# A graph layer with a mixture of experts on one core: three sweeps over the experts with carried places, and results weighed by ScalarE

## What is computed

```python
def layer(x, src, dst, edge_weight, ...):        # x: 3125 x 256, float32; 53125 edges, sorted by dst
    support = layernorm(x) @ weight               # 256 x 256
    msgs = support[src] * edge_weight[:, None]
    x = x + segment_sum(msgs, dst) + bias
    y = layernorm(x)
    top_w, top_i = top_k(y @ Wg + bg, 2)          # 8 experts, each row goes to two
    top_w = softmax(top_w)
    for e in range(8):                            # W1: 256 x 1024, W2: 1024 x 256
        h = gelu(y @ W1[e] + b1[e])
        x = x + w_dense[:, e:e+1] * (h @ W2[e] + b2[e])
    return x
```

## Time and profile before

| | us |
|---|---|
| median of 3 runs | 967.78 |
| lowest, highest | 967.74, 975.76 |
| the profiled execution, time | 968.8 |
| the profiled execution, span from first to last instruction | 967.0 |

### The profile page before, as it was taken

One profiled execution on the slowest core, in us unless ns is written; L12 is line 12 of the kernel. 1 busy time (PEld: TensorE's weight loads), 2 busy tenths in 40 slices (PEclk: granted clock), 3 DMA queues, 4 the chain that ended last, 5 costly groups with the idle time before them and its releaser, 6 DMA issues.

```text
span 967.0 us, 16433 instructions
## 1 busy us (share of the span) xinstructions
PE 783.5 (81%) x5365; PEld 764.0 (79%) x5365; DVE 424.2 (44%) x1229; ACT 307.8 (32%) x594; POOL 585.8 (61%) x570
## 2 busy tenths in 40 slices
PE   1076769966975865399999999999996999999994
PEld 0075768866875764399999999899985999999994
DVE  6422223321331336033655376254634466566653
ACT  5200100200100000124433425344732466666652
POOL 4477777777777777777777777704005255555422
PEclk9999999999999999999999899899988999999998
DMA  8888789753465494436465564714213465666632
GB/s 210 249 291 291 254 270 296 208 158 106 140 175 154 116 267 129 119 116 223 118 222 162 187 189 149 243 42 132 76 55 104 115 164 130 157 173 174 168 56 39
DMA packets 104892, 160.22 MB, mean 166 GB/s; under 512 B 18146, under 2 KB 82131, under 8 KB 104680
## 3 DMA queue, kind: packets, MB, share of 16 engines
q0 software_dynamic: 34688, 69.13, 26.4%
q1 hardware_dynamic: 53988, 64.24, 22.4%
q10 hardware_dynamic: 16132, 25.81, 8.3%
HBM read 107.42 MB, written 51.61 MB: 164 GB/s over the span
## 4 chain that ended last, share of the span: by engine, by line
PE 63%; POOL 11%; DMA 10%; DVE 7%; issue 6%; ACT 1%; DVEq 0%; ACTq 0%; POOLq 0%; SPq 0%
PE ps_agg L786 20%; PE ps_o L948 19%; PE ps_h L931 17%; POOL G L578 7%; DMA G<-xn_d,src_t 7%; POOL y_d L591 3%; PE ps_m L843 2%; DVE w_lo L1143 2%; PE ps_o L852 2%; PE ps_y L904 1%; PE ps_y L843 1%; DMA xe_int<-in_src 1%; DMA y_d<-yr,pos_i 1%; DVE G L1413 1%; DVE ost L1342 1%
## 5 line engine op out<-in xcount | busy, mean ns | idle before, releaser
L578 POOL DMA_INDIRECT G<-xn_d,src_t x416 | 417.2, 1003 | 147.0 <-issue 116.2
L786 PEld LDWEIGHTS ps_agg<-S,G 128*128 128x128 f32 x1664 | 295.1, 275 | 93.0 <-issue 85.2
L786 PE MATMUL ps_agg<-S,G 128*128 128x48 f32 x1664 | 297.8, 354 | 86.1 <-DMA G<-xn_d,src_t 84.3
L728 ACT ACTIVATE hf<-ps_h,b_t 128x256 f32<-128x256 f32 x272 | 113.4, 468 | 231.3 <-PE ps_h L931 206.1
L931 PE MATMUL ps_h<-y_hi,w_hi 128*128 128x256 f32 x544 | 161.5, 297 | 3.3 <-DVE y_lo L1324 3.3
L1330 DVE TENSOR_TENSOR h_lo<-hf,h_hi 128x512 fp32r<-128x512 f32 x136 | 93.3, 692 | 157.4 <-ACT h_hi L731 156.0
L931 PE MATMUL ps_h<-y_hi,w_lo 128*128 128x256 f32 x544 | 157.6, 290 | 0.0
L931 PE MATMUL ps_h<-y_lo,w_hi 128*128 128x256 f32 x544 | 156.8, 288 | 0.0
L1111 DVE TENSOR_TENSOR S<-iota_w,rel_t 128x192 f32<-128x192 f32 x104 | 36.9, 361 | 209.7 <-PE ps_agg L786 202.2
L622 POOL DMA_INDIRECT result<-ost,add_i x34 | 57.7, 1698 | 111.1 <-DVE ost L1347 103.9
L948 PE MATMUL ps_o<-w_hi,h_hi 128*128 128x256 f32 x544 | 114.1, 291 | 9.2 <-DVE h_lo L1330 9.1
(11 more groups left out here) (163 smaller groups left out, 630.6 us busy)
## 6 DMA issues: line engine op xcount, KB each, us to landing
w_raw<-in_L_ffn_W ACTq DMA_DIRECT2D x24, 1024.0 KB, 7.7
y_d<-fill SPq DMA_DIRECT2D x14, 896.0 KB
y_d<-fill SPq DMA_DIRECT2D x14, 777.0 KB
G<-xn_d,src_t POOLq DMA_INDIRECT x416, 3.7
yg<-y_d SPq DMA_DIRECT2D x19, 259.0 KB, 3.6
yg<-y_d SPq DMA_DIRECT2D x19, 256.0 KB, 2.8
y_d<-ost SPq DMA_DIRECT2D x17, 256.0 KB
w_raw<-in_L_ffn_W SPq DMA_DIRECT2D x4, 1024.0 KB, 15.1
```

The lines of the kernel that those rows point to most:

```text
L578: pool.indirect_dma_start(G[:, k, :], None, xn_d, bass.IndirectOffsetOnAxis(src_t[:, n, c:c + 1], 0)).then_inc(main.gathered[n % NR], 16)
L728: nc.scalar.activation(hf[:, j % 2, m, :], ps_h[:, j % 2, m * T:(m + 1) * T], ACT.Gelu, bias=b1_t[:, e * KH + c:e * KH + c + 1]).then_inc( ...
L786: return nc.tensor.matmul(ps_agg[:, k // GT % 2, m * WIN:(m + 1) * WIN], G[:, k, m * 128:(m + 1) * 128], S[:, k, :], start=start, stop=stop)
```

## The change

The nodes are in three sets, `((4, 3, 2), (4, 4), (4, 2, 2))`. The first two sweeps do exactly one tile per expert (16 visits): what an expert has over 256 rows stays in the table and is taken up by the next sweep (`run` is carried over, and only raised where an expert has less than its tile). The third sweep does all the rest, at least one tile an expert. All 16 visits are written out and need no numbers from the chip; `sweep_tables` runs once, for the third sweep.

Every tile now carries node and gate weight (`tile_marks` for all). The results of the visits 0 to 14 are multiplied with the gate weight by ACT in the first quarter of the next tile (`weigh`), and stored by SP to a table `r_d`. SP loads them later into the ring G, free by then, and POOL adds them to the output: visits 0 to 4 (`OLD[0]`) between the send of the last chunk but one and the last, visits 5 to 14 in the third sweep, one or two per expert (`OLD_AT`). The combining of set 0 (L610 to L617, L1406 to L1415) is gone. In the third sweep a tile's results are treated after the first step of the next tile, and an expert's weights are split after its predecessor's last tile.

```diff
-CHUNK_BLOCKS = ((4, 4, 3, 2), (4, 4, 4))
+CHUNK_BLOCKS = ((4, 3, 2), (4, 4), (4, 2, 2))
...
+    STILL = len(SETS) - 1
+    NV = STILL * X
+    AHEAD = NV - 1
...
-    PAIRS_AT = (4, 4, 4, 4, 4, 3, 0, 0)
+    PAIRS_AT = (3, 3, 3, 3, 3, 2, 2, 2, 2, 3, 2, 2, 1, 0, 0, 0)
+    LINEAR_AT = {v: CHUNKS[L0 + n] for n, v in enumerate((3, 5, 9, 11, 13))}
+    TURN_AT = {v + 1: c for v, c in LINEAR_AT.items()}
-    SEND_AT = [COMPLETE[c.index] + pairs_beside(c) + 2 for c in CHUNKS[:L0 - 2]] + [U0, U0 + 2]
-    SEND_AT += [min(HEAD_U[e + 1] + 3, NP) for e in TURN_AT]
+    SEND_AT = [COMPLETE[c.index] + pairs_beside(c) + 2 for c in CHUNKS[:L0 - 1]] + [U0 + 1]
+    SEND_AT += [min(HEAD_U[v + 1] + 1, NP) for v in TURN_AT]
+    OLD = (range(0, 5), range(5, AHEAD))
+    OLD_AT = [[v for v in OLD[1] if (v - OLD[1][0]) * X // len(OLD[1]) == i] for i in range(X)]
...
@@ SP @@
+            for v in range(NV):
...
+                if v < X:
+                    fill_rows(sp, SETS[2], v)
+                new_sweep = (v + 2) % X == 0
+                if not new_sweep and v < AHEAD:
+                    place_free(v + 1)
+                    load_tile(first_rows(v + 2))
+                if v < AHEAD:
+                    store_result(v)
+                if HEAD_U[v] == NP and HEAD_U[v - 1] < NP:
+                    sp.wait_ge(main.used, RING + NG * GT)
+                    sp.wait_ge(q.stored, (v + 1) * 16)
+                    load_old(0)
+                if new_sweep:
+                    rows_sent(SETS[(v + 2) // X])
+                    place_free(v + 1)
+                    load_tile(first_rows(v + 2))
...
@@ POOL @@
+            def add_old(n, v):
+                pool.wait_ge(s_old[n], 16 * len(OLD[n]))
+                pool.wait_ge(s_old_i[n], 1)
+                pool.wait_ge(s_old_added, 16 * TH * v)
+                for h in range(TH):
+                    pool.indirect_dma_start(out, bass.IndirectOffsetOnAxis(old_i[:, v, h:h + 1], 0),
+                                            G[:, v * TH + h, :], None, compute_op=ALU.add).then_inc(s_old_added, 16)
...
             for c, a, z in zip(CHUNKS, [0] + SEND_AT, SEND_AT):
                 gather_pairs(a, z)
+                if c is CHUNKS[-1]:
...
+                    for v in OLD[0]:
+                        add_old(0, v)
                 send(c)
...
+            for i, e in enumerate(SWEEP[STILL]):
+                first, end = bounds(pool, e)
+                for h in range(TH):
+                    pool.wait_ge(q.added[h], first * 16)
+                pool.sem_inc(s_go, 1)
+                for v in OLD_AT[i]:
+                    add_old(1, v)
+                pool.wait_ge(s_old_added, 16 * TH * (OLD_AT[i][-1] + 1))
+                with pool.Fori(first, end) as r:
+                    add_tile(r - 1)
+            add_tile(end - 1)
...
@@ ACT @@
+            def weigh(v):
+                act.wait_ge(q.biased, v + 2)
+                act.wait_ge(q.meta, v * 4 + 4)
+                for h in range(TH):
+                    nc.scalar.activation(ost[:, h, :], ost[:, h, :], ACT.Identity,
+                                         scale=w_tab[:, v, h:h + 1]).then_inc(q.weighed, 1)
...
@@ DVE, place_rows @@
+                for s in SETS[:STILL]:
+                    if c is s.last:
+                        own(V.scalar_tensor_tensor(out=run[:, :], in0=room_row[:, :], scalar=float((s.index + 1) * T),
+                                                   in1=run[:, :], op0=ALU.add, op1=ALU.max))
...
@@ DVE, third sweep @@
+                with dve.Fori(first, end) as r:
+                    g = r + AHEAD
+                    hidden_low(g, 0)
+                    results_to_add(r - 1)
+                    for j in range(1, NQ):
+                        hidden_low(g, j)
+                    tile_low(g + 1)
```

More of the change, by code:

```diff
@@ L48, with __init__ @@
 class NodeSet:
-    def __init__(self, index, chunks, tile, experts):
+    def __init__(self, index, chunks, nodes_up_to, tile):
         self.index, self.chunks = index, chunks
[L53 to L56, removed]
+        self.last = chunks[-1]
+        self.room = index + -(-nodes_up_to // tile)
 class ChunkSems:
@@ new lines, in rows_sent, with first_rows, place_free, store_result @@
+            def rows_sent(s):
+                for c in s.chunks:
+                    sp.wait_ge(ch.sent[c.index], 32 * c.blocks)
+            def first_rows(v):
+                row = (VISITS[v] * ROOM + v // X) * T
+                return slice(row, row + T)
+            def place_free(n):
+                sp.wait_ge(q.tile_t, n + 1)
+                sp.wait_ge(q.meta, n * 4 + 3)
+            def store_result(v):
+                sp.wait_ge(q.weighed, (v + 1) * TH)
+                sp.dma_start(r_d[v * T:(v + 1) * T, :].rearrange("(h p) d -> p h d", p=128),
+                             ost[:, :, :]).then_inc(q.stored, 16)
@@ new lines, in _ @@
+            sp.wait_ge(q.route, 1)
+            row = tile_row(2)
+            place_free(NV)
+            load_tile(bass.ds(row, T))
+            sp.wait_ge(q.stored, NV * 16)
+            load_old(1)
+            for e in SWEEP[STILL]:
+                first, end = bounds(sp, e)
+                with sp.Fori(first, end) as r:
+                    row = tile_row(r + 2)
+                    place_free(r + AHEAD + 1)
+                    load_tile(bass.ds(row, T))
+            sp.wait_ge(q.tile_in, (end + AHEAD + 2) * 16)
@@ L509, in _ @@
+            sp.sem_inc(s_over, 1)
             for done in ch.stored:
                 sp.wait_ge(done, 32)
[L511 to L512 removed]
         @block.gpsimd
@@ new lines, in _ @@
+            act.wait_ge(q.route, 1)
+            for i, e in enumerate(SWEEP[STILL]):
+                v = NV + i
+                first, end = bounds(act, e)
+                with act.Fori(first, end) as r:
+                    hidden(e, r + AHEAD)
+                    tile_high(r + NV)
+                if is_new(v + 2):
+                    act.wait_ge(q.hidden, (end + AHEAD) * NQ)
+                    load_raw(act, LOADS[v + 2], 1)
+                if is_new(v + 1):
+                    split_high_all(v + 1)
+                if is_new(v + 2):
+                    act.wait_ge(q.result, end + AHEAD)
+                    load_raw(act, LOADS[v + 2], 2)
@@ L984, in _ @@
+            pe.wait_ge(q.route, 1)
+            for i, e in enumerate(SWEEP[STILL]):
+                load = LOADS[NV + i]
+                first, end = bounds(pe, e)
+                pe.wait_ge(s_split1, STEPS * (load + 1))
+                with pe.Fori(first, end) as r:
+                    tile(load, r + AHEAD)
         @block.vector
@@ new lines, in _ @@
+            dve.wait_ge(q.meta, NV * 4)
+            old_nodes(1)
+            dve.wait_ge(q.stored, NV * 16)
+            for i, e in enumerate(SWEEP[STILL]):
+                v = NV + i
+                first, end = bounds(dve, e)
+                with dve.Fori(first, end) as r:
+                    g = r + AHEAD
+                    hidden_low(g, 0)
[3 more added lines that the diff above has]
+                    tile_low(g + 1)
+                if is_new(v + 1):
+                    for which in (1, 2):
+                        for n in range(STEPS):
+                            split_low(LOADS[v + 1], which, n)
```

772 lines of the change are left out of this document (332 added, 440 removed).

## The result

The changed kernel took 1008.96 us (median of 4 runs, 1007.8 to 1010.33), the kernel before 967.83 beside it: 1.040 times as long, 95% interval 1.035 to 1.045. I had forecast 985 us, slower by 1.8%; it is slower by 4.0%: 41 us where I had said 17, inside the range of 945 to 1012 and outside that of my own case, 970 to 1000.

A forecast was written before the change was run, and what follows sets the result against it. Before, POOL's gathers bound until 631 us, PE from 404.4. Forecast: visit 12 done at 688, tile 14 at 712, last send 759.3, third sweep from 780, plus 166.2 and 22.5, then the end: 983 + 1.8 = 985 us; range 945 to 1012.

The forecast's parts named there:

- my own case: Whole kernel: the summed forecast of 985 us, with a range of 970 to 1000; chance 0.40.
- the supply of groups in the two sweeps: First two sweeps: POOL needs 1.30 us per gather, 10.4 per pair; gathers done at 667, visit 12 at 688.
- visit 13: End of the second sweep: 20.5 us after visit 12's end plus 3.3 for turn and gate; tile 14 starts at 712.
- the adds and weights of the third sweep: Third sweep: old adds that delay results and six changes of weights cost 22.5 us together.
- 30 tiles: All sweeps: 30 tiles instead of 34, four times 11.86, 47 us of PE gone.
- POOL's waits for places: Sends in the first two sweeps: POOL waits for places about 3, 14 and 11 us.
- its largest term: Before the last send: POOL adds five old tiles one after another, four trips 27.6 us; send at 759.3, third sweep at 780.
- Rival 1: First two sweeps: PE keeps up with POOL, its 28 us of waits go; 951 us; chance 0.17.
- Rival 2: Switch and third sweep: the add queue is short, trips of 5.6 us, 20 less; 965 us, no change; chance 0.23.
- rival 3: Sweeps: clock stays low longer; spells of 15 us, visit 12 ends at 712, 1009 us; chance of this part 0.17.
- Its second part: All the sweeps at half clock: visit 12 would end at 868, 1165 us; chance 0.03.
- the three stretches from there to the third sweep: Tile 14's start to first old add 15.9 us, to last send 31.4, to the third sweep's first tile 20.7.

The follow-up runs named there:

- experiment 5: Changed kernel with DVE instead of ACT multiplying the stored results, right behind the bias: 995.06 us, ratio 1.026 to the kernel before.
- experiments 1 to 3: Each against the changed kernel: last chunk sent before the five old adds, 998.28 us; five old results loaded a visit earlier, 985.61; 15 stored results not added, 959.21.
- experiment 7: Changed kernel with ten old results loaded in visit 12, five added before the last send, five right behind it, five in the third sweep: 984.73 us, ratio 1.012.
- experiments 8 and 9: Changed kernel with wider margins at two sends, ten old results loaded in visit 11, adds spread: 1132.51 us, ratio 0.969; same with DVE multiplying: 1132.42, 0.970.
- 12: Changed kernel with the third set's rows filled ahead of the first tile instead of in visits 0 to 7: 1185.53 us beside 1153.54 of the kernel before.
- 13: Changed kernel with the third set's rows filled ahead of the first tile, run again: 1195.05 us beside 1152.13 of the kernel before.
- experiments 14 and 15: On one chip: changed kernel with the third set's rows filled ahead of the first tile, 1003.06 us, ratio 1.035; changed kernel as it is, 1002.40, 1.033.
- experiment 10: Changed kernel with wider margins at two sends, ten old results loaded in visit 11, adds spread, ACT multiplying, on another chip: 956.76 us, ratio 0.985.

## Why the prediction was off, step by step

**The step that failed.** It was the size of three terms of the sum, not the mechanism: the supply of groups in the two sweeps (a gather at 1.30 us, where it cost 1.34), visit 13 (24 us, where it took 30, with a wait on `ps_m` that the sum did not have), and the adds and weights of the third sweep (22.5 us, where they cost 31.8). A rise of 41 us came where 17 had been forecast.

**Right.** 30 tiles: 480 matmuls per group. POOL's waits for places at three sends: 4.1, 14.7 and 10.8, forecast 3, 14 and 11. How close these came is partly luck: in the second profile of the same kernel they are 8.5, 18.7 and 12.1. The first tile's first matmul came at 303.4, forecast 299; its send was 4 us late and the 14 from there on right. From the start of tile 14 (727.5) to the first old add 14.3, forecast 15.9. From there to the last send 30.5, forecast 31.4; a trip 6.7, forecast 6.9. From that send to the third sweep's first tile 18.9 (772.3 to 791.2), forecast 20.7. ACT's place in front of the store: 8.4 in experiment 5, forecast 9. The mechanism of the forecast, and its largest term, stand; experiments 1 to 3 show it.

**Mis-sized, in order of time.** The span was forecast at 983 and is 1005.8, 22.8 more. All of this is read from the one trace; only the gathers were tried in runs of their own.

The end of the gathers: 682.6 instead of 667, though the waits were right. POOL's groups between 291 and 683 us, after and, to 632, before:

```profile
L589 POOL DMA_INDIRECT G<-xn_d,src_t x240 | 249.1, 1038 | 73.1 <-issue 54.8 <-PE ps_agg L828 18.3
L601 POOL DMA_INDIRECT y_d<-yr,pos_i x27 | 33.0, 1223 | 37.0 <-DVEq L1250 29.6 <-issue 7.3
```

```profile
L578 POOL DMA_INDIRECT G<-xn_d,src_t x229 | 230.4, 1006 | 69.8 <-issue 51.5 <-PE ps_agg L786 18.0 <-DVEq L1228 0.3
```

A gather with its gap cost (249.1 + 73.1) / 240 = 1.34 us, not the 1.30 of "I take 1.30": 10 us. Before, the same window gives 1.31, a mean over a stretch without tiles and one with them; the sweeps begin earlier now, so all of it is the dearer kind. The term was a mean over two regimes where one of them had been asked for, and the prediction had its price: 1.33, from 396 to 631 us. With it 7 of the 10 us would have been in the sum. Three more send instructions fell in the window than I had counted (27, not 24), as the first tile's send was late: 4 us; the waits 1.6 more. 9 of these 15.6 reach the end of visit 12 (697.4, not 688): it comes 14.8 us behind the last gather, not 21.

Visit 13: 30 us to the start of tile 14 where I had 24. The last chunk's linear waited 5.1 us for DVE, which came to the ranks of the chunk before, in the same buffer (`ps_m`), only behind two weight steps: a wait on a buffer that the sum did not have. The other 1.0 stays unexplained.

The third sweep: 14 transposes from 796.97 to 982.94 are 186.0 us, 31.8 above 13 x 11.86, where I had 22.5 in all for adds and weights. The wait at tile 17 was 13.0, not 10.7; expert 4's two adds cost 10.9, not 4, since the second took 10.4 us (901.20 to 911.57) instead of 6.9; the last tile lost 2.6, weights 3.5 instead of 6. Together 9.3 over the forecast of the stretch. From the last result to the end it took 16.6 instead of 14.3.

Sum: 9.4 at visit 12 and 6.1 in visit 13; less 4.3 for the three stretches from there to the third sweep, each a little shorter than forecast (1.6, 0.9 and 1.8); 9.3 in that sweep and 2.3 behind it: 22.8.

**The rivals.** Rival 1, that PE keeps up, is refuted by the waits at the sends. Rival 2's trips of 5.6 did not come. Of rival 3 the time came close (1009), but not for its reason: visit 12 ended at 697, not 712. Its slow spells are there in part: after the 15.5 us wait for tile 8 the granted clock read 0.50 from 549.5 to 561 us, some 12 us where I had counted 8. Its second part, half clock in all the sweeps, did not come: 0.86 in the mean from 300.75 to 697.4. The spell of 404 to 419 us in the kernel before, from which I took the 15, shows only in the durations (12 matmuls in 2.92 us); the profile gives 1.00 as the granted clock there. The Trainium skill, "DMA: Bandwidth & Descriptors" (Anatomy of one DMA), whose fixed 2.0 us and bytes at 436 GB/s would by my estimate have made a trip 1.8 us shorter, is not borne out for these accumulating transfers: they took 4.0 us to land in the median, 3.7 at least, and a trip was 6.7 at the switch, 7.6 in experiment 7.

**The range** for my own case, 970 to 1000, took the errors of the terms as if they fell on both sides. The large ones fell on one: the three terms above came out 9.4, 6.1 and 9.3 too small, and what was too large, the three stretches around the switch, gave back 4.3.

## What to carry to other kernels

Serial work that is parked "for later" must be laid against the time in which its engine is idle, piece by piece: here 15 adds of 7 us cost 43 to 50 us in one order, and with ten of their loads two visits earlier, the adds spread over POOL's idle stretches and a wider margin at two sends the kernel beats the one before by 1.5%. A queue that is only moved behind the thing that it delayed delays the next thing. A transfer's place in its issuing engine's queue counts as much as its own wait: the multiplication on ACT cost nothing that could be measured but the loads that stood behind its store.

## What the runs showed of the hardware that I had not expected

In three of the comparisons every kernel ran slower by a fifth: the kernel before took 1163.94 (experiments 8 and 9), 1153.54 (12) and 1152.13 us (13) there, instead of 966 to 971. The record gives chips 15, 11 and 4 for them, and it gives chip 11 again for experiments 14 and 15, ten minutes after 12, where the kernel before took 968.59. So it need not be a property of the chip. The engines' work hardly differs between experiments 8 and 10: PE was busy for 764.1 and 735.1 us, DVE for 429.3 and 428.3, ACT for 320.0 and 319.9, POOL for 589.5 and 597.6. What grows is idle time that the profile puts down to no engine of this core (`remote`); experiment 8's waits, and beside them POOL's in experiment 10, which has none on `remote`:

```profile
DVE S L1145 <- remote: 208.4, 19, 34.8
...
POOL y_d L601 <- DVEq L1256: 108.9, 7, 43.3
```

```profile
POOL y_d L601 <- DVEq L1256: 37.8, 4, 14.6
```

Why is open; no run here tests it. It moves ratios too (0.969 there against 0.985), so such a ratio is not mixed with the others.

PE came back from 33 us of idleness faster than I had allowed for. The four transposes at 783.68 took 1.11 us, those at 982.94 took 0.60. The granted clock read 0.50 up to 786, 0.81 from 786 to 788 and 1.00 from there; the first tile of the third sweep began 6.4 us after the transposes (784.8 to 791.2), where I had put 8.5.
